# Two adaLN blocks on one core: fp32 scores in four row groups, and the causal mask of the turned scores as a minimum on VectorE

## The reference, cut to what matters

```
qkv_heads = qkv.reshape(b, heads, s, -1)
q, k, v = jnp.split(qkv_heads, 3, axis=-1)
qk = jnp.einsum('bhse,bhte->bhst', q, k) * scale
mask = jnp.triu(jnp.full((s, s), -jnp.inf, dtype=jnp.float32), k=1)
attn = jax.nn.softmax(qk + mask, axis=-1)
out = jnp.einsum('bhst,bhte->bhse', attn, v).reshape(b, s, e)
```

## Time and profile before

| | |
|---|---|
| median of 3 runs | 2192.94 us (2183.0 to 2194.02) |
| profiled execution, its time | 2209.41 us |
| profiled execution, its span | 2207.7 us |
| TensorE products busy | 2023.7 us, 92% |
| VectorE busy | 1552.6 us, 70% |
| ScalarE busy | 735.9 us, 33% |
| mean granted clock | 0.92 |

### The profile page before, as it was taken

How to read it: one execution, slowest core, us unless ns; L and a number is a source line. 1 busy time by engine, 2 the same in 40 slices (tenths; PEclk the granted TensorE clock), 3 DMA queues, 4 the chain that set the end, 5 groups by cost and what they waited for, 6 DMA issues and landing times.

```text
span 2207.7 us, 36821 instructions
## 1 busy us (share of the span) xinstructions
PE 2023.7 (92%) x12681; PEld 1502.5 (68%) x12681; DVE 1552.6 (70%) x3759; ACT 735.9 (33%) x1447; POOL 68.9 (3%) x78
## 2 busy tenths in 40 slices
PE   1457799999999999999999999999999999999998
PEld 1233567777776767677686767777676777777776
DVE  6356475968777685868868586877868696876464
ACT  0121415242332525243342514344252424333331
POOL 0000000000000000000000000000000000000000
PEclk9865779998997989899899979999897999999899
DMA  4011200203030200303020020303021030202000
GB/s 123 22 40 50 77 20 20 75 10 91 11 91 11 77 20 5 91 11 91 11 87 14 23 68 11 91 11 91 11 63 33 6 91 12 84 12 77 12 13 5
DMA packets 130096, 97.17 MB, mean 44 GB/s; under 512 B 28000, under 2 KB 124512, under 8 KB 125824
## 3 DMA queue, kind: packets, MB, share of 16 engines
q1 hardware_dynamic: 121536, 91.74, 14.5%
q10 hardware_dynamic: 8448, 4.20, 0.7%
HBM read 56.48 MB, written 29.98 MB: 39 GB/s over the span
## 4 chain that ended last, share of the span: by engine, by line
PE 73%; DVE 17%; issue 5%; ACT 2%; DMA 1%; SPq 1%; DVEq 1%; POOL 0%; ACTq 0%; POOLq 0%
PE y_ps L1419 13%; PE b_bank L1315 13%; PE b_bank L1311 5%; PE up_ps L1412 4%; PE gate_ps L1412 4%; PE b_bank L1379 3%; PE a_bank L1170 3%; PE gate_ps L1414 3%; PE gate_ps L1413 3%; PE up_ps L1413 3%; PE up_ps L1414 3%; DVE mneg L1051 3%; PE a_bank L1285 2%; PE b_bank L1170 2%; DVE h L1146 2%
## 5 line engine op out<-in xcount | busy, mean ns | idle before, releaser
L1419 PE MATMUL y_ps<-wd,h 128*128 128x128 f32 (+1 forms) x3072 | 414.0, 284 | 1.3 <-DVE mixed L1133 0.4
L1419 PEld LDWEIGHTS y_ps<-wd,h 128*128 128x128 f32 (+1 forms) x3072 | 382.6, 195 | 44.7 <-issue 20.7
L777 ACT ACTIVATE tt<-gate_ps 128x512 f32<-128x512 f32 x352 | 210.8, 599 | 603.6 <-PE gate_ps L1414 576.3
L1138 DVE SCALAR_TENSOR_TENSOR tt<-tt,gate_ps 128x512 f32<-128x512 f32 x352 | 240.0, 682 | 148.4 <-ACT tt L777 145.3
L1146 DVE TENSOR_TENSOR h<-tt,up_ps 128x512 f32<-128x512 f32 x352 | 239.8, 681 | 85.0 <-PE up_ps L1414 66.9
L737 ACT ACTIVATE arena<-b_bank 128x512 f32<-128x512 f32 x384 | 209.3, 598 | 232.8 <-PE b_bank L1315 232.7
L1051 DVE TENSOR_REDUCE mneg<-b_bank 128x2 f32<-128x512 f32 x256 | 164.6, 684 | 39.6 <-PE b_bank L1315 37.1
L1412 PE MATMUL up_ps<-h_hi,wu_hi 128*128 128x512 f32 x352 | 178.7, 508 | 7.1 <-DVE h L1146 6.0
L1412 PE MATMUL gate_ps<-h_hi,wg_hi 128*128 128x512 f32 x352 | 165.9, 471 | 16.5 <-DVE h_lo L1113 10.1
L1315 PE MATMUL b_bank<-k_stack,q_stack 24*128 24x128 f32 (+1 forms) x1024 | 173.9, 449 | 0.0
L1315 PE MATMUL b_bank<-q_stack,k_stack 26*128 26x256 f32 (+1 forms) x1024 | 173.4, 445 | 0.0
(11 more groups left out here) (189 smaller groups left out, 2933.0 us busy)
## 6 DMA issues: line engine op xcount, KB each, us to landing
q_stack<-q_rows SPq DMA_DIRECT2D x16, 1024.0 KB, 5.4
k_stack<-k_rows SPq DMA_DIRECT2D x16, 1024.0 KB, 7.6
q_rows<-qk_halves SPq DMA_DIRECT2D x48, 256.0 KB, 3.1
k_rows<-qk_halves SPq DMA_DIRECT2D x48, 256.0 KB, 3.7
rows<-mod_rows SPq DMA_DIRECT2D x48, 128.0 KB, 3.2
rows<-mod_rows SPq DMA_DIRECT2D x16, 384.0 KB, 4.8
x_in<-in_L_attn_X SPq DMA_DIRECT2D x16, 256.0 KB, 7.8
vals<-arena SPq DMA_DIRECT2D x128, 32.0 KB, 2.1
```

The lines of the kernel that those rows point to most:

```text
L777: send(a(tt[:, ch % 2, :], gate_ps[:], ACT.Tanh, scale=0.5), tanh_ready)
L1138: send(v.scalar_tensor_tensor(tt[:, ch % 2, :], tt[:, ch % 2, :], 1.0, gate_ps[:], ALU.add, ALU.mult), g_free)
L1419: ins = mm(y_ps[:, P * t:P * (t + 1)], h32[rows_, ch % 3, P * t:P * (t + 1)], wd[rows_, ch, :], start=first and t == 0, stop=last_ and t = ...
```

## The change

The scores are computed in fp32 with the 8 rows of a head alone: `ROWS`, the split halves, the stores to DRAM and `m_hi`/`m_lo` are gone. `q32` and `k32` are copied straight from one place in SBUF to another. A unit now takes four row groups at once (`GROUPS`), in four banks: 6 units of `maxima` and 6 of `rows`. In the wide ones (names B and E) each group has two heads of 256 columns, in the narrow ones (A and L) four of 128. The maxima still begin with the mask product; the turned scores have none. Instead VectorE takes, after the exponential, the minimum of the probabilities and a table `keep_k` of 0 and 3e38 (`cover`). Seven PSUM banks are one pool now, and a table `USES` gives each use its bank; the gate and up products are in it. The tables of the order are new for all engines; the first two gate products and swishes stand a turn earlier, and the last downs at the end of their own turn.

```diff
-ROWS = 3 * HD
+HUGE = 3.0e38
-COUPLES = NHP // 8
-UNITS = 3 * COUPLES
-PROBS = 4
+GROUPS = 4
+HTILE = NHP // GROUPS
+EARLY = ("E0", "E1", "E2", "E3")
+SCORES = ("A0", "B0", "B1", "A1", "B2", "B3")
+TURNED = ("E0", "L0", "E1", "E2", "L1", "E3")
+PROBS = 3 * GROUPS
+USES = [(0, "eg2", "D", 3), (0, "eu2", "D", 2), (0, "eg3", "D", 6), (0, "eu3", "D", 4), (0, "eg4", "D", 1), (2, "G0", "D", 3),
...
-            def stack(it):
-                if it.earlier():
-                    sp.wait_ge(rb.ready.sem, rb.ready.at(it.earlier(), rb.k(f"TC{2 * COUPLES - 1}")))
-                sp.wait_ge(halves_stored.sem, halves_stored.at(it, 6))
-                for dst, src in ((q_stack, q_rows), (k_stack, k_rows)):
-                    send(sp.dma_start(dst[:].bitcast(F32), src.rearrange("g r c x -> (g r) c x")), stacked)
+            def stack(it, k):
+                src, dst, use = ((q32, q_stack, "LQ"), (k32, k_stack, "LK"))[k]
+                sp.wait_ge(*ps.is_freed(it, use))
+                for g in range(GROUPS):
+                    send(sp.dma_start(dst[32 * g:32 * g + HD, :, :], src[:, P * g:P * (g + 1)]), stacked)
...
-            v.tensor_scalar(mask_k[:], code_rowf, code_col[:], NEG, ALU.is_lt, ALU.mult)
+            v.tensor_scalar(keep_k[:], code_rowf, code_col[:], HUGE, ALU.is_ge, ALU.mult)
...
+            def cover(it, u):
+
+                dve.wait_ge(*ps.is_freed(it, f"T{TURNED[u]}{GROUPS - 1}"))
+                n = S if TURNED[u] in EARLY else P
+                x = probs[:, GROUPS * (u % 3):GROUPS * (u % 3 + 1), :].rearrange("p g (h k) -> p (g h) k", k=n)[:, :, 0:P]
+                send(v.tensor_tensor(x, x, keep_k[:].unsqueeze(1).to_broadcast([P, GROUPS * 512 // n, P]), ALU.min), covered)
...
             def maxima(it, u):
-                q, kind = u // 3, u % 3
+                name = SCORES[u]
+                wide, n = name[0] == "B", int(name[1])
                 if u == 0:
-                    after(it, stacked, 2)
-                use = {g: f"S{'ABC'[kind]}{g}" for g in couple(q)}
-                for g in couple(q):
-                    masked(it, use[g], mask_q, by_key(use[g], P) if kind == 0 else by_key(use[g], S)[:, :, P:S], 2 if kind else 4)
-                heads = 2 if kind else 4
+                    after(it, stacked, 2 * GROUPS)
+                use = [f"S{name}{g}" for g in range(GROUPS)]
+                for g in range(GROUPS):
+                    masked(it, use[g], mask_q, by_key(use[g], S)[:, :, P:S] if wide else by_key(use[g], P), 2 if wide else 4)
+                heads = 2 if wide else 4
...
             def rows(it, u):
...
-                for g in couple(q):
-                    masked(it, use[g], mask_k, by_key(use[g], P) if kind == 2 else by_key(use[g], S)[:, :, 0:P], 2 if kind < 2 else 4)
-                heads = 2 if kind < 2 else 4
+                use = [f"T{name}{g}" for g in range(GROUPS)]
+                for g in range(GROUPS):
+                    free(it, use[g])
+                heads = 2 if wide else 4
                 for j in range(heads):
+                    for g in range(GROUPS):
+                        h = HTILE * g + heads * n + j
+                        if wide:
+                            last = mm(ps.bank(use[g])[:, S * j:S * (j + 1)], stack_cols(k_stack, HD + 1, h, 0), stack_both(q_stack, HD + 1, h),
+                                      start=True, stop=True)
...
-            def weigh(it, q):
+            def weigh(it, w):
...
+                ue, ul = TURNED.index(f"E{w}"), TURNED.index(f"L{w // 2}")
+                after(it, covered, max(ue, ul) + 1)
+                free(it, f"W{w}")
...
```

More of the change, by code:

```diff
@@ L214, in owned, with __init__, signal_ready, signal_freed @@
-def owned(uses, who):
-    return sum(1 for _, w in uses if w == who)
+class Banks:
+    def __init__(self, banks, signal):
+        self.banks = banks
+        self.place = {name: n for n, (_, name, _, _) in enumerate(USES)}
+        leads = sorted({lead for lead, _, _, _ in USES})
+        self.ready = {lead: signal(f"ready_{lead}", sum(1 for use in USES if use[0] == lead)) for lead in leads}
+        self.freed = {}
+        self.nth_ready, self.nth_freed = {}, {}
+        for lead in leads:
+            mine = [use for use in USES if use[0] == lead]
+            for n, (_, name, who, _) in enumerate(mine):
+                self.nth_ready[name] = n + 1
+                self.nth_freed[name] = sum(1 for use in mine[:n + 1] if use[2] == who)
+            for who in sorted({use[2] for use in mine}):
+                self.freed[lead, who] = signal(f"freed_{lead}_{who}", sum(1 for use in mine if use[2] == who))
+    def bank(self, name):
+        return self.banks[USES[self.place[name]][3]]
+    def signal_ready(self, name):
+        return self.ready[USES[self.place[name]][0]]
+    def signal_freed(self, name):
+        lead, _, who, _ = USES[self.place[name]]
+        return self.freed[lead, who]
+    def is_ready(self, it, name):
+        s = self.signal_ready(name)
+        return s.sem, s.at(it, self.nth_ready[name])
+    def is_freed(self, it, name):
+        s = self.signal_freed(name)
+        return s.sem, s.at(it, self.nth_freed[name])
+    def turned_over(self, it, name):
+        n = self.place[name]
+        lead, _, _, bank = USES[n]
+        for back in range(1, (FIRST + LAST + 1) * len(USES)):
+            turn, at = divmod(n - back, len(USES))
+            old_lead, old, _, old_bank = USES[at]
+            if old_bank != bank:
+                continue
+            before = Turn(it.reg, it.plus - lead + turn + old_lead)
+            if it.reg is not None or 0 <= before.plus < PAIRS:
+                return self.is_freed(before, old)
+        return None
@@ L413, in turn @@
                 order(do)
-            for plus in range(-FIRST, LAST):
+            for plus in range(-FIRST, LAST + 1):
                 turn(None, plus)
-            with eng.Fori(0, PAIRS - FIRST - LAST) as it:
-                turn(it, LAST)
+            with eng.Fori(0, LOOPS) as it:
+                turn(it, LAST + 1)
             for plus in range(PAIRS - FIRST, PAIRS + LAST):
@@ L1004, in quantise_h @@
                 if k == 0:
-                    own(it, ra2.freed["D"], ra2.nth[f"U{2 * half + 1}"])
+                    done(it, f"U{2 * half + 1}")
                     block_scales(step, src, n)
@@ L1297, in query1 @@
+                free(it, use)
+                send(mm(ps.bank(use)[:], wl_s[:, r, :], h3t, start=True, stop=True), ps.signal_ready(use))
             def query1(it):
-                evacuated(it, ra2, "T3")
                 project(it, 0, "LQ")
@@ L1345, in turn_max @@
-                send(last, rb.ready)
+                    last = mm(ps.bank("MT")[0:NH, 2 * NHP * t:2 * NHP * (t + 1)], ident[:, t:P:8], mneg[:], start=True, stop=True)
+                send(last, ps.signal_ready("MT"))
             def rows(it, u):
-                q, kind = u // 3, u % 3
+                name = TURNED[u]
+                wide, n = name in EARLY, int(name[1])
                 if u == 0:
-                    after(it, m_stacked, 8)
-                use = {g: f"T{'ABC'[kind]}{g}" for g in couple(q)}
@@ L1423, in down @@
             def down(it, ch):
-                after(it, h_ready, ch + 1)
+                evacuated(it, f"eu{ch}")
                 pr, j = ch // PAIRCH, ch % PAIRCH
```

695 lines of the change are left out of this document (322 added, 373 removed), and 30 rows, old and new, of tables (B_USES, USES).

## The result

The changed kernel takes 2173.5 us (median of 19 runs, 2161.8 to 2185.3) against 2192.9 for the kernel before (19 runs, 2175.5 to 2207.2): a ratio of 0.992, 95% interval 0.990 to 0.995. It is faster by 17 us (0.8%), 12 to 23 by the interval, where 103 were forecast. All ratios here are to the kernel before, run beside the other on the same chip. The profiled execution took 2164.2 us with a span of 2162.2.

A forecast was written before the change was run, and what follows sets the result against it. TensorE was taken as the bound, busy 92% of the span. From 2209 us profiled, -112 on TensorE and +10 for VectorE gave 2107, or 2090 us as median (57%, 2060 to 2125); range 2015 to 2200.

The forecast's parts named there:

- the wide units take 4 x 0.217 + 0.29 = 1.16 us: Score products on TensorE: four groups' loads go side by side at 0.217 us a pass; all score units -46 us.
- The half-clock rows: Profile rows: score loads last 302 and 301 ns at full and half clock, taken to show that groups load side by side.
- rival 1: All twelve score units a pair: only two groups' loads go side by side, a pass 0.434 us; about 2300 us, slower; 11%.
- The point from which it decides: Score passes on TensorE: 64 a pair may cost 0.334 us each before the whole gain is lost.
- Rival 3: All score units: loads wait for their own group's product, +99 us in place of -46; 2227 us; 5%.
- rival 5: Whole kernel: nothing gained, since an equal loss elsewhere cancels the mask products that leave; 2193 us; 3%.
- Rival 2: Weighing waits behind VectorE because the minimum lies half on the path; +4.7 us a pair, +71, 2161 us; 14%.
- The mask products, -63 us: TensorE, turned scores: mask products go, 73 us in all, less 10 us for changes of row groups that stay.
- The minimum, +10 us: VectorE: 9.5 us a pair of minima, free in the second half; +10 us charged for waits and the first half.
- The filling: Pipeline start: the first pair's scores gain nothing as TensorE waits anyhow, so 15/16 of -119 us counts, -112.
- Pairs at 118 to 120 us, TensorE over 95% busy: Sign that the forecast holds: pairs of samples this far apart, with TensorE still over 95% busy between.
- Rival 4: First half of each pair: low-clock stretches go with the maxima's small units, a further 74 us; 2016 us; 10%.

## Why the prediction was wrong, point by point

**The forecast's term "the wide units take 4 x 0.217 + 0.29 = 1.16 us" failed**, and it alone costs the expected gain. They take 2.03 us, 8 x 0.87 = 7.0 us a pair more, against the 7.4 us a pair of TensorE's whole sum. The step behind it: as lower bound of a pass I took "the product itself", 0.24 us for 256 columns, from the tails of products that are made in one pass of fp32r, and carried it over to passes of fp32. An fp32 pass over the same spaced columns takes 0.43 us, beyond the load step under which I had it hidden. The two figures did not fit even as they stood: the 0.217 us taken for a wide pass lay under the 0.24 called its lower bound. That neighbouring columns bring a wide unit to 1.07 us, near the forecast, does not bear the forecast out: there the load step itself is no longer 0.217 us.

**The half-clock rows were read half.** I saw in the earlier trace rows that the score loads do not slow down at half clock, and concluded that they go side by side. They do: rival 1 fell, and the narrow unit came out at 2.03 us for 1.91. But a time that does not change with TensorE's clock is not the clocked array's, and the run with neighbouring columns, which does change with the clock (1.07 and 2.02 us), shows that here it was the reading of the spaced operands. I wrote that the columns lie 16 elements apart and left it at the loads; the moving operand lies just so. The section of the Trainium skill named above ("Advanced Engine Details and Errata", SBUF Cachelines) was the rule to weigh there.

**The point from which it decides came out, in part by luck.** By the forecast 64 passes a pair may cost 0.334 us each before all is lost. Half of them cost 0.43 and half about 0.22, a mean of 0.33, and the pair takes what it took. But that point was worked out with 4.0 us a pair for the mask products and nothing for idle time, and both are off, in opposite directions (below). The price in the wide units was rival 1's 0.434, by another cause. Rival 3 comes nearest in its mechanism, loads that wait for a product of their group, and its 0.457 us for a wide pass is near the 0.43. That is chance: it adds a load step to a product of 0.24 us, while the load ran beside a product of 0.43. Its narrow pass, 0.337 us, was about 0.22.

**The direction, faster, was right in part by luck.** In the pairs, where the forecast had the whole gain, there is none (126.6 us for 125.9). Of the outcomes named, rival 5 fits best, an equal loss elsewhere, which had 3%. Rival 2's 2161 us is nearest in number, but the wait on which it rests was 9.7 us in the whole run.

**The mask products, -63 us** (59 in fifteen pairs): the direction was right, the size too small. Alone on the kernel before they are worth 83 us, 6.3 us a pair in the profiles (125.9 - 119.6) for the 4.0 reckoned; from 400 to 1700 us the granted clock was 0.98 there and 0.93 in the kernel before, which is the likely rest and was not tested by itself. Added up, the two measured sizes come near the whole: units of 2.03 us make 12 x 2.03 = 24.4 us a pair for the 19.8 of before, +4.6, 15 times +69; 69 - 83 = -14, and 12 to 23 less were measured. It is an addition of two runs on different orders, not a run of its own, and stretch by stretch it does not close: in the pairs it gives 4.6 - 6.3 = -1.7 us, where +0.7 was measured, with 3.2 us a pair more of idle TensorE, and the filling, which it leaves out, gave 43. The forecast's sum had no term for that idle time; it held that the shared banks could only give.

**The minimum, +10 us**: right that it is hidden, and it cost nothing that the runs can tell (2180 us without it, 2174 with it). VectorE came to 101.6 us a pair for 101.8, the minima to 1.22 and 2.29 us for 1.22 and 2.3. But that it is hidden is the order's doing: in the kernel before, with my own places for it, it cost 84 us.

**Fewer changes of mode, -10 us**, was not measured by itself. **The filling**, to which I gave nothing (the factor 15/16), is where the profiled gain lies: 43 us, at a granted clock of 0.81 for 0.76. TensorE's waits in the filling of the kernel before name one part, the key halves on their way through DRAM:

```profile
PE b_bank L1311 <- DMA k_stack<-k_rows: 10.9, 1, 10.9
```

In the kernel before without the mask products, the filling was 12 us shorter (261.4 us), at a clock of 0.84. What the remaining time was is left open.

**Pairs at 118 to 120 us, TensorE over 95% busy**: wrong, 126.6 us and 95%. Rival 4 did not occur in the changed kernel either, where the clock was 0.93 to 0.97 in the eight pairs.

## What to carry to other kernels

Before a product's time is taken for the array's, look at how far apart its operands' elements lie, and look for the same line at the other clock level: a time that stays is not set by the array alone; here it was that of reading the operands. Elements 64 bytes apart doubled the score units at full clock, and giving ScalarE, which was idle two thirds of the time, 6 us a pair of rearranging shortened a pair from 126.6 to 117.0.
A price that is carried over holds only for the same number of passes and the same type: the 0.24 us taken from fp32r was 0.43 in fp32.
Work that is put on a queue with room costs by its place in the queue: the same kind of minimum cost 0 us and 84, and three activations cost 57 us more in one place than in another.

## What was not expected of the hardware

- Spaced operands (one element every 64 bytes) take 0.43 us for 256 columns a pass in fp32 at full clock, and the unit takes 2.03 us at both clock levels; in neighbouring elements, or in runs of 8, the unit takes 1.1 to 1.2 us at full clock and, in neighbouring elements at half clock, again 2.02. Loads of 128 such columns take 0.30 us against 0.19.
- TensorE took products of other row groups ahead of those issued before them: with the groups issued one after the other, all four still started together in the wide unit of 4 passes a group (2.05 us for 2.03); in the narrow one of 8 passes a group the order cost (5.18 for 2.03).
- With the products of two groups cut to 8 columns the wide unit was no shorter, the granted clock over eight pairs was 0.91 for 0.96, and the kernel was 46 us slower than with all the work.
